# Layer three of a gated feed-forward block in Strassen's form, in passes woven between the steps of layers one and two

## The reference

```
x = x + tanh(g_xattn) * (softmax(Q K^T / sqrt(32)) V Wo + bo)     # Q from layernorm(x), K and V from ctx, 16 heads
h = concat([n, -n]), n = layernorm(x)
h = relu(s0 * h @ sign(k0)) * 2       # layer one:   1024 -> 2048
h = relu(s1 * h @ sign(k1)) * 2       # layer two:   2048 -> 2048
h =      s2 * h @ sign(k2)            # layer three: 2048 -> 512
x = x + tanh(g_ffn) * h
```

## Time and profile before

| | us |
|---|---|
| median of 3 runs | 1567.62 (1564.46 to 1568.11) |
| profiled execution, its own time | 1564.91 |
| its span | 1563.1 |
| PE busy | 1518.9 |
| DVE busy | 940.2 |
| ACT busy | 673.7 |

### The profile page before, as it was taken

How to read it: one execution, slowest core, us unless ns; L and a number is a source line. 1 busy time by engine, 2 the same in 40 slices (tenths; PEclk the granted TensorE clock), 3 DMA queues, 4 the chain that set the end, 5 groups by cost and what they waited for, 6 DMA issues and landing times.

```text
span 1563.1 us, 46137 instructions
## 1 busy us (share of the span) xinstructions
PE 1518.9 (97%) x19872; PEld 1297.3 (83%) x19872; DVE 940.2 (60%) x1938; ACT 673.7 (43%) x1568; POOL 168.7 (11%) x273
## 2 busy tenths in 40 slices
PE   6798999999999999999999999999999999999999
PEld 4586888888888888898988888888898888889887
DVE  5877766756556565655656566465655656565442
ACT  3452452635435253452535445263553525345231
POOL 2202001010100102011020200101010010201000
PEclk9999999999999999999999999999999999999999
DMA  9443232342424333252443524333242443424100
GB/s 256 127 104 58 46 95 62 89 70 62 90 52 101 65 85 78 50 100 55 96 69 71 93 44 103 62 89 69 62 90 52 101 67 83 78 50 100 29 29 15
DMA packets 278227, 120.96 MB, mean 77 GB/s; under 512 B 243464, under 2 KB 259848, under 8 KB 277896
## 3 DMA queue, kind: packets, MB, share of 16 engines
q1 hardware_dynamic: 275960, 117.48, 34.6%
q10 hardware_dynamic: 2064, 0.53, 0.1%
HBM read 37.76 MB, written 16.78 MB: 35 GB/s over the span
## 4 chain that ended last, share of the span: by engine, by line
PE 80%; DVE 8%; ACT 6%; issue 3%; DMA 2%; POOL 0%; SPq 0%; ACTq 0%; DVEq 0%; POOLq 0%
PE bank L1255 19%; PE bank L1256 19%; PE bank L1222 7%; PE bank L1223 7%; PE bank L1272 6%; PE bank L1273 6%; ACT Pf L529 3%; DVE nmax L804 2%; PE bank L1139 2%; PE bank L1141 2%; PE bank L1140 2%; PE bank L1123 2%; PE bank L1124 2%; PE bank L1125 2%; DMA PT<-Phl 1%
## 5 line engine op out<-in xcount | busy, mean ns | idle before, releaser
L1255 PE MATMUL bank<-H,W 128*128 128x128 f16 x6720 | 778.3, 219 | 5.7 <-ACT C L622 4.4
L1256 PE MATMUL bank<-H,W 128*128 128x128 f16 x6720 | 778.0, 219 | 0.0
L1255 PEld LDWEIGHTS bank<-H,W 128*128 128x128 fp8e5 x6720 | 655.3, 98 | 18.1 <-ACT C L622 10.2
L1256 PEld LDWEIGHTS bank<-H,W 128*128 128x128 fp8e5 x6720 | 657.4, 98 | 7.1
L1222 PE MATMUL bank<-hT,W 128*128 128x256 f16 x1024 | 226.8, 273 | 3.5 <-DVE hT L745 1.9
L1223 PE MATMUL bank<-hT,W 128*128 128x256 f16 x1024 | 226.8, 273 | 0.0
L529 ACT ACTIVATE Pf<-bank,nmax 128x128 f32<-128x128 f32 x512 | 146.4, 368 | 137.1 <-DVE nmax L804 135.4
L1273 PE MATMUL bank<-W,h 128*128 128x512 fp8e5 x504 | 191.0, 379 | 0.0
L1272 PE MATMUL bank<-W,h 128*128 128x512 fp8e5 x504 | 191.0, 379 | 0.0
L476 POOL TENSOR_TENSOR attn<-pvs 128x128 f32<-128x128 f32 x120 | 75.0, 625 | 1002.9 <-DVE pvs L817 1002.9
L844 DVE TENSOR_TENSOR C<-bank,C 128x256 f32<-128x256 f32 x180 | 76.3, 424 | 159.4 <-ACT C L622 87.8
(11 more groups left out here) (133 smaller groups left out, 1910.3 us busy)
## 6 DMA issues: line engine op xcount, KB each, us to landing
Qst<-q_bounce SPq DMA_DIRECT2D x120, 128.0 KB, 2.8
Y<-in_x_dram SPq DMA_DIRECT2D x16, 512.0 KB, 3.9
R<-X SPq DMA_DIRECT2D x16, 512.0 KB, 3.5
q_bounce<-Qhl SPq DMA_DIRECT2D x120, 64.0 KB
out_dram<-R SPq DMA_DIRECT2D x15, 512.0 KB, 2.6
W<-in_L_ffn_k_dram SPq DMA_DIRECT2D x8, 512.0 KB, 8.1
W<-in_L_ffn_k_dram SPq DMA_DIRECT2D x2, 1024.0 KB, 19.3
PT<-Phl SPq DMA_TRANSPOSE x120, 3.1
```

What stands on the lines that cost most here:

```text
L1255: mm(o, w, H0[:, 0, i, b_of, :], start=first, stop=False, skip_group_check=True)
L1256: last = mm(o, w, H0[:, 1, i, b_of, :], start=False, stop=i == PAIRS - 1, skip_group_check=True)
```

## The change

Layer three gets Strassen's form too, from chunk 1 on. Two groups make one pass p (groups 0 and 1, or 2 and 3): seven steps of 8 matmuls of 256 columns (`third_step`), in banks 3 and 4 by turns. After a step DVE adds the bank to a quarter of `R` at once (`add_up`, eight reads a pass). Pass 0 lies in slots 31 to 42 of the same chunk, between the steps of L1 of group 2; pass 1 lies in slots 4 to 15 of the next chunk, between the pairs of L0. `SLOTS` grows to 50.

For it the output of layer two must be there in seven rows instead of four quarters: ACT rectifies into `Fp` (`rectify`), DVE makes three sums a group (`group_sums`), ACT converts five and then two rows, 1,280 and 512 elements a partition (`group_hi`), DVE makes the rests of these (`group_lo`); both stand in the slot of P1 of the next group, ACT's before the copy of C11. They replace `h1_rest`.

In L1 the order is now P1, P2, P6, P5, P7, P3, P4, P3 opens bank B anew, which makes a fourth sum a group, and the roles A, B, C move on by one bank from group to group (`ROLES`). PE at the first step of a pass waits for `h2_lo` of the early rows, at the second for the late ones.

The attention items lie in other slots. The sums of signs of `W2` are made in chunk 1 (LATE_WEIGHTS, group 4). In the last chunk groups 2 and 3 are fed to L2 plainly, with a part of `W2` restored. To find the room in SBUF, `Pf` has one buffer instead of two, `attn` shares `xn`, `Qf` shares `pvs`, `ident` and two buffers of the first phase share others, and `Kst` holds one batch of keys (the second is loaded in chunk 7).

The core of the diff, lines left out at "...":

```diff
     A, B, C = range(3)
     STEPS = [(A_L11, B_R11, A, True), (A_L12, B_R21, B, True), (A_S2, B_T2, A, False),
-             (A_S1, B_T1, C, True), (A_S3, B_T3, A, False), (A_L22, B_T4, A, False),
-             (A_S4, B_R22, C, False)]
-    P1, P2, P6, P5, P7, P4, P3 = range(7)
+             (A_S1, B_T1, C, True), (A_S3, B_T3, A, False), (A_S4, B_R22, B, True),
+             (A_L22, B_T4, A, False)]
+    P1, P2, P6, P5, P7, P3, P4 = range(7)
+    ROLES = [[(q + role) % 3 for role in range(3)] for q in range(GROUPS)]
...
+    PASS = [(A_L11, H_R11), (A_L12, H_R21), (A_S2, H_T2), (A_S1, H_T1), (A_S3, H_T3), (A_S4, H_R22), (A_L22, H_T4)]
+    PASS_BANK = [3, 4, 3, 4, 3, 4, 3]
+    READS = [(P1, 0, 1), (P2, 0, 1), (P6, 0, 0), (P5, 1, 0), (P5, 0, 0), (P7, 1, 0), (P3, 0, 0), (P4, 1, 1)]
+    PASS_NEEDS = [0, 0, 1, 2, 3, 5, 6]
+    READ_NEEDS = [0, 1, 0, 0, 3, 4, 5, 0]
...
+    PLAIN_FEED = {0: {0: (0, 0), 1: (0, 1), 3: (1, 0), 4: (1, 1)}, 1: {0: (2, 0), 1: (2, 1), 2: (3, 0), 3: (3, 1)}}
...
-    LAST_FEED = [(1, 0, 1), (1, 1, 2), (0, 1, 0), (0, 0, 3)]
-
-    SLOTS = [("L0", i, 0) for i in range(PAIRS)] + [("L2P", GROUPS - 1, h) for h in range(2)]
-    for q in range(GROUPS):
-        SLOTS += [("L1", q, s) for s in (P1, P2, P6, P5, P7)]
-        SLOTS += [("L2", q - 1, h) for h in range(2)] if q else []
-        SLOTS += [("L1", q, s) for s in (P4, P3)]
+    LAST_FEED = [(0, 1, 0), (1, 0, 1), (0, 0, 2), (1, 1, 3)]
+    SLOTS = [("L0", i, 0) for i in range(4)]
+    for n in range(4):
+        SLOTS += [("L2", 1, n), ("L0", 4 + n, 0)]
+    SLOTS += [("L2", 1, P7), ("L2", 1, P3), ("L1", 0, P1), ("L2", 1, P4)] + [("L1", 0, s) for s in range(P2, 7)]
+    SLOTS += [("L1", 1, s) for s in range(7)] + [("L1", 2, P1), ("L1", 2, P2)]
+    for n, s in enumerate((P6, P5, P7, P3)):
+        SLOTS += [("L2", 0, n), ("L1", 2, s)]
+    SLOTS += [("L2", 0, P7), ("L2", 0, P3), ("L1", 2, P4), ("L2", 0, P4)] + [("L1", 3, s) for s in range(7)]
...
-    for u in range(U):
-        weave(10 + 2 * u, "S", u)
-        weave(11 + 2 * u, "PS", u)
-        weave(15 + 2 * u, "PV", u)
+    for u, (scores, values) in enumerate(((14, 20), (17, 22), (19, 24), (21, 26), (23, 28), (25, 31), (27, 33),
+                                          (29, 36))):
+        weave(scores, "S", u)
+        weave(scores + 1, "PS", u)
+        weave(values, "PV", u)
     for t in range(TT):
-        weave(28 + 2 * t, "CT", t)
-        weave(31 + 2 * t, "WO", t)
-        weave(32 + 2 * t, "N2", t)
-        weave(33 + 2 * t, "T2", t)
-    weave(31, "LOAD", 0)
+        weave(34 + 3 * t, "CT", t)
+        weave(40 + 2 * t, "WO", t)
+        weave(41 + 2 * t, "N2", t)
+        weave(42 + 2 * t, "T2", t)
+    weave(39, "LOAD", 0)
     for t in range(TT):
-        weave(36 + t, "LN", t, 2)
-        weave(38 + t, "N1", t, 2)
-        weave(39 + t, "T1", t, 2)
+        weave(43 + t, "LN", t, 2)
+        weave(45 + t, "N1", t, 2)
+        weave(46 + t, "T1", t, 2)
...
+    LATE_WEIGHTS = ({9: (0, 0), 16: (1, 0), 18: (0, 1), 21: (0, 2), 23: (2, 0), 25: (0, 3), 26: (1, 1), 27: (0, 4),
+                     29: (1, 2), 32: (3, 0), 36: (1, 3), 38: (1, 4), 41: (2, 1), 44: (2, 2), 46: (2, 3), 48: (3, 1)},
+                    {13: (2, 4), 17: (4, 1), 20: (4, 2), 24: (4, 3), 30: (3, 2), 34: (4, 4), 38: (3, 3), 41: (3, 4)})
...
+            def group_hi(q, f):
+                for n, rows in enumerate((EARLY_ROWS, LATE_ROWS)):
+                    act.wait_ge(h2_step, 3 * group(f, q) + 2 + n)
+                    if n == 0:
+                        act.wait_ge(*pass_free(f, q))
+                    nc.scalar.activation(h1[:, q % 2, 0, :, rows, :], Fp[:, 1:3, rows.start + 1:rows.stop + 1, :],
+                                         ACT.Copy).then_inc(h2_hi, 1)
...
                 if kind == "L1":
                     if s == P1:
...
+                        if n > 0 and not late(f, n - 1):
+                            group_hi(n - 1, f)
...
+                        take(n, s, f, C11)
                     if s == P2:
...
+                        act.wait_ge(l1_sum, nth(f - 1, NC, 4 * n))
+                        if n == 0:
+                            act.wait_ge(l0_lo, nth(f, NP, NP - 1))
+                        elif not late(f, n):
+                            act.wait_ge(h2_lo, 2 * group(f, n))
+                        rectify(n, f, 0, H_R11 + 1, C11[:, :, :])
                     if s == P6:
...
+                        if late(f, n - 1):
+                            act.wait_ge(h1_lo, NH + 3)
+                        take(n, s, f, C12)
                     if s == P7:
...
+                        if late(f, n - 1):
+                            act.wait_ge(h1_lo, NH + 2)
+                        take(n, s, f, C22)
+                    if s == P3:
+                        act.wait_ge(l1_sum, nth(f - 1, NC, 4 * n + 2))
+                        rectify(n, f, 1, H_R22 + 1, C22[:, :, :])
                     if s == P4:
+                        act.wait_ge(l1_sum, nth(f - 1, NC, 4 * n + 3))
+                        rectify(n, f, 2, 0, C12[:, :, :])
                         act.wait_ge(l1_done, nth(f, NL1, 7 * n + s))
...
+            def group_sums(q, f):
+                done = 3 * group(f, q)
+                Fg = Fp[:, 1:3]
+                dve.wait_ge(h2_relu, 3 * group(f, q) + 3)
+                V_.tensor_tensor(Fg[:, :, 3:5, :], Fg[:, :, 1:3, :], Fg[:, :, 0:1, :].to_broadcast([P, 2, 2, HALF]),
+                                 ALU.subtract).then_inc(h2_step, 1)
+                dve.wait_ge(h2_step, done + 1)
+                V_.tensor_tensor(Fg[:, :, 5, :], Fg[:, :, 4, :], Fg[:, :, 1, :], ALU.add).then_inc(h2_step, 1)
+                dve.wait_ge(h2_step, done + 2)
+                dve.wait_ge(l1_copy, copied(f, q, 3))
+                V_.tensor_tensor(Fg[:, :, 7, :], Fg[:, :, 6, :], Fg[:, :, 5, :], ALU.subtract).then_inc(h2_step, 1)
+            def group_lo(q, f):
+                for n, rows in enumerate((EARLY_ROWS, LATE_ROWS)):
+                    dve.wait_ge(h2_hi, 2 * group(f, q) + n + 1)
+                    V_.tensor_tensor(h1[:, q % 2, 1, :, rows, :], Fp[:, 1:3, rows.start + 1:rows.stop + 1, :],
+                                     h1[:, q % 2, 0, :, rows, :], ALU.subtract).then_inc(h2_lo, 1)
+            def add_up(f, p, s):
+                base = NR * passes(f, p)
+                for n, (step, half, tile) in enumerate(READS):
+                    if step != s:
+                        continue
+                    if n == 0 and p == 0:
+                        dve.wait_ge(r_copied, nth(f, 16, 15))
+                    if READ_NEEDS[n]:
+                        dve.wait_ge(l2_sum, base + READ_NEEDS[n])
+                    dve.wait_ge(l2_step, 7 * passes(f, p) + s + 1)
+                    rest = R[:, tile, half * CHUNK:(half + 1) * CHUNK]
+                    V_.scalar_tensor_tensor(out=rest, in0=banks[PASS_BANK[s]][:, 0:CHUNK], scalar=fin, in1=rest,
+                                            op0=ALU.mult, op1=ALU.add).then_inc(l2_sum, 1)
...
+                if kind == "L2" and f - n >= 1:
+                    add_up(f - n, n, s)
...
+                    banks_of = ROLES[n]
+                    if s == P1 and n > 0 and not late(f, n - 1):
+                        group_lo(n - 1, f)
                     if s == P2:
...
+                        dve.wait_ge(l1_copy, copied(f, n, 0))
+                        add(n, s, f, C11, banks_of[B])
+                    if s == P6 and late(f, n):
+                        last_rest(n, 0, C11[:, :, :])
+                    if s == P5:
+                        dve.wait_ge(l1_copy, copied(f, n, 1))
+                        add(n, s, f, C12, banks_of[C])
                     if s == P7:
...
+                        dve.wait_ge(l1_copy, copied(f, n, 2))
+                        add(n, s, f, C22, banks_of[C])
                     if s == P3:
...
+                        dve.wait_ge(l1_sum, nth(f - 1, NC, 4 * n + 1))
+                        add(n, s, f, C12, banks_of[B])
+                        if late(f, n):
+                            last_rest(n, 1, C22[:, :, :])
+                    if s == P4 and late(f, n):
+                        last_rest(n, 2, C12[:, :, :])
+                        last_rest(n, 3, banks[banks_of[A]][:, 0:CHUNK].rearrange("p (j n) -> p j n", j=2))
+                    if s == P4 and not late(f, n):
+                        group_sums(n, f)
...
                     if s == P1 and n > 0:
-                        pe.wait_ge(h1_lo, nth(f, NH, 4 * (n - 1) + 2))
-                    if s == P2 and n > 0:
-                        pe.wait_ge(l1_sum, nth(f - 1, NC, 3 * (n - 1)))
+                        pe.wait_ge(l1_sum, nth(f - 1, NC, 4 * (n - 1) + 3))
                     if s == P6:
-                        pe.wait_ge(l1_copy, nth(f - 1, NC, 3 * n))
-                    if s == P5 and n > 0:
-                        pe.wait_ge(l1_sum, nth(f - 1, NC, 3 * (n - 1) + 2))
```

(35 more changed lines are left out.)

320 lines of the change are left out of this document (181 added, 139 removed).

## The result

The changed kernel takes 1642.54 us (median of 4 runs, 1640.23 to 1643.11) against 1567.31 us for the kernel before (4 runs). The ratio is 1.0481, interval 1.0462 to 1.0499: slower by 75 us. The forecast was slower by 43 us, 1611 us with a range to 1628. So the sign is right and the size is not. The profiled execution took 1643.0 us.

What follows compares the result with a forecast made beforehand. PE's matmul order was taken as the bound, with ACT and DVE's 0.4 us slack a round deciding. 1564.9 - 23.1 - 9.1 + 57.4 + 14.3 + 6 - 0.4 = 1610.0, plus 1: 1611 us, forecast range 1592 to 1628, wider range 1562 to 1628.

Steps and rivals of the forecast that it cites:

- The undisturbed period: Regular chunk at full clock, first pair to next chunk's first pair: forecast 95.7 us, 92.66 us in the kernel before.
- What bounds the kernel: Steady state: PE, busy 97%, sets the time by its matmul order; a change is worth its columns and waits.
- the slack of 0.4 us a round: Attention exchange in L1 of groups 0 and 1: ACT and DVE need 3.63 us a round, PE 4.04 us.
- Columns, -0.80 us a pass: Layer three: 56 matmuls of 256 columns replace 32 of 512, 6.11 for 6.91 us; 29 passes give -23.1 us.
- Old waits, -0.65 us a chunk: Short waits before P4 and P6 vanish with rotating banks and P4 after P3: -9.1 us over 14 chunks.
- The walk through groups 0 and 1, +4.1 us: PE waits at P6 (1.37) and P7 (0.8) of group 1 and slot 31 (1.93 us): +57.4 us in 14 chunks.
- The chunk's end, 1.1 us: P4 of group 3 waits 0.4 us, the first L0 step 0.7, behind N1 and T1: +14.3 us over 13 chunks.
- The clock: Rival "more waiting": a 2 us PE wait in every chunk could lower the clock; above 1628 us, chance 0.05.
- Chunk 0 costs nothing: Chunk 0, among other parts of the change, costs nothing that PE waits for: 0 us.
- Chunk 1, +6 (2 to 9) for the `W2` sums: Chunk 1 also makes W2's four sums; about 9.5 us before slot 31 meet some 4 us of slack.
- the 4 us of slack: Chunk 1 before slot 31: slack set against about 9.5 us of sums of signs, leaving +6 us.
- First phase, nothing: Aliases in the first phase cost nothing that PE waits for; PE there waits for attention, which they don't lengthen.

Runs made afterwards that it cites:

- the narrow groups: Changed kernel with group sums, conversions and rests on 16 of 128 columns, output left incomplete: 1547.96 us, ratio 0.9874.
- the banks alone: Kernel before, layer three not in Strassen's form, with only P3 before P4, a fourth C sum a group and rotating banks: 1561.76 us, ratio 0.9966.
- the part on GpSimd: Changed kernel with the third group sum and the rest of the late rows moved from DVE to GpSimd: 1630.88 us, ratio 1.04.
- the pass later: Changed kernel with pass 0 starting one L1 step later, behind P6 of group 2: 1624.14 us, ratio 1.0361.
- all four edits: Changed kernel with pass 0 one step later, chunk 0's sums of signs earlier, third sum and late rests on GpSimd, score items moved: 1601.08 us, ratio 1.021.
- the copy first: Changed kernel with ACT's C11 copy of the next group ahead of the two group conversions: 1662.87 us, ratio 1.0605.
- the chunk's end earlier: Changed kernel with the layernorm items LN, N1 and T1 one slot earlier: 1642.29 us, ratio 1.0481.
- the sums in chunk 0: Changed kernel with W1 sums earlier, plus three W2 sums of signs moved from chunk 1 to chunk 0: 1639.23 us, ratio 1.0451.
- the one with a gap of 1.76 us: Changed kernel with group operations on 16 of 128 columns, plus a PE gap before slot 31 from six GpSimd additions: 1579.59 us, ratio 1.0076.

## Why the prediction was right in sign and wrong in size

The waits and their places were right; the size failed in four terms. A lower clock behind slot 31 and any loss in chunk 0 were put at nothing and cost 9.6 and 3.9 us. The sums of signs in chunk 1 were put at 6 us and cost 12. The undisturbed period was put at +2.95 us a chunk and came out at +3.75. Another 3.25 us go with the execution. By its own steps:

- **What bounds the kernel: right.** PE's order sets the time, and the slack of 0.4 us a round on ACT and DVE decides.
- **Columns, -0.80 us a pass: right** (-1.55 us for two passes, from the narrow groups against the banks alone). The weights stay hidden: a step of a pass still takes 0.87 us.
- **Old waits, -0.65 us a chunk: right** (92.00 for 92.66).
- **The walk through groups 0 and 1, +4.1 us: nearly right.** P6 1.36 for 1.37, P7 0.81 for 0.8, slot 31 2.30 for 1.93. The prices of the unseen operations were 1.27 (1.270 measured) and 1.48 us (1.545). The third stop came out 0.37 too small.
- **The chunk's end, 1.1 us: 1.39** (0.46 and 0.93). With slot 31 and the columns (0.05 less than forecast) that is 0.7 of the 0.8 us by which an undisturbed chunk is longer than the terms say (+3.75 for +2.95); 0.1 has no place found. Over 13 chunks it is about 10 us. (The prediction's period of 95.7 us is 95.6 by its own terms.)
- **The clock: the step that failed in kind.** The fall behind the slot-31 wait was named as a rival and set aside, since the first 20 us of the kernel before, with PE busy for 8.84, show 1.00. That row stands for the launch and not for a gap inside a stream. Six chunks at 1.6 us make 9.6 us; the part on GpSimd, which has no such fall, is shorter by just that in chunks 2 to 14. The Trainium skill (TensorE: Matmul & The Clock Gate, HAM oscillation — how this bites in real kernels) tells of a kernel whose waits for data send the clock to its lower level time and again. The runs here show the same behind gaps of PE of 1.95 us and more, and behind none of 42 gaps of 1.91 us or less.
- **"Chunk 0 costs nothing": wrong by 3.9 us.** It had 3.45 us less for PE to do, and ran no shorter. The `W1` sums at slots 44 to 48 stand before the rest that PE's first L0 step needs, and that wait is 5.9 us for the 1.6 of the kernel before. Moved forward they gave back 2.2 us of the 3.9 in chunk 0 (3.0 with chunk 1); after that PE waits for `xT`.
- **Chunk 1, +6 (2 to 9) for the `W2` sums: 12 measured.** Chunk 1 makes eight sums of signs; the five in slots 13 to 30 are three of `W2` and two of `W1`. P6 of group 1 waits 3.97 us in it, with the lower clock behind. The step that failed is the 4 us of slack set against these sums. The narrow groups keep the sums of signs and have next to no work for the rows, and their chunk 1 still takes 101.07 us, where their undisturbed chunk, with one pass in Strassen's form in place of two, would take 90.45 + 0.80. So the signs cost 9.8 us there, with waits of 1.0, 1.5 and 1.9 us and one fall of the clock, and 109.89 - 96.41 - 0.80 = 12.7 us with the rows at full width. The likely reason, which no run tests by itself, is that a sum of 2.3 us comes in one piece and is longer than the slack between two hand-offs. With three of them taken out, chunk 1 was 3.2 us shorter.
- **First phase, nothing:** +3.25 us, in this execution. It shows a clock of 0.96 there for the 1.00 of the kernel before, and the kernel with the banks alone has 0.95 and +2.0, while the runs with the pass later and with all four edits have no such delay (73.8 us at clock 1.00). It goes with the execution and not with the change.

In chunks 2 to 14 the clock (9.6) and the longer period (10.4) make 20 us, of which about 1 comes back in chunk 14 and in shorter waits for DMAs. 3.25 + 3.9 + 6.1 + 19.0 + 0.95 = 33 us, the distance from 1610.0 to 1643.0. The structure of the waits was read rightly from the trace before. The forecast's range was too narrow at the top because each term was summed at its middle, while what a full chain adds (the clock behind a long wait, an operation longer than the slack it falls into) only ever added here.

## What to carry to other kernels

Saving columns on a TensorE that is 97% busy pays only if the operations that feed the new form fit between the others' hand-offs: walk one period of the serving engines in order, at the place where they are fullest, and don't go by their mean share. When the walk finds a wait of TensorE of about 2 us or more, add the clock behind it (here 1.6 us in half of the cases at 2.1 us), and first move the step until the wait is split or gone: with the pass one slot later chunks 2 to 14 took 19.8 us less, 11 by the waits and most of the rest by the clock. Compare a long operation with the one gap that it falls into, not with the sum of the slack around it. Moving a delay within a chain that is full (the copy first, the chunk's end earlier, the sums in chunk 0) gave it back elsewhere in all three runs. Work handed to GpSimd is priced with what it takes from VectorE while both run.

## What the runs showed of the hardware

- Idle times of TensorE of 1.10 to 1.91 us, once a period of 90 to 99 us, left the granted clock at 1.00 in 42 of 42 chunks. Of 2.08 to 2.15 us, 23 of 45 were followed by a lower clock, of 2.52 us 9 of 11, of 2.92 to 3.08 us 12 of 13. In the rows shown 4.6 us from the pass's first step on are at 0.63, a mean of a part at full and a part at half speed (the two levels are 2.4 and 1.2 GHz). A fall cost 1.6 us.
- On GpSimd the rest of 512 elements took 1.80 us in the mean, where its addition of 512 from `Y` and `bo_b` takes 1.27 us and DVE needs 0.68. The 14 that overlap DVE's N1 took 1.16 us (and N1 1.37), the 44 beside DVE's rest of the early rows or a sum in `Fp` took 1.94 us or more.
- The other way round, a DVE sum of 256 elements from SBUF took 0.42 us, and 1.38 us where it overlapped GpSimd's rest (14 of 14).
- A layernorm step of one element a partition on GpSimd (`var_eps`) took 0.26 us in the mean in the kernel before, 0.86 us in the changed one and 0.20 in the one with a gap of 1.76 us. The traces show what it overlaps. It takes 0.19 us alone or beside a DVE sum that reads a PSUM bank (L844, 14 of 14), 0.54 us beside DVE's group sum (L957) and 1.34 us beside its rest of 1,280 elements (L968), 14 times each. So DVE's new operations hold it up, and a mean over all its cases hides that. In the kernel with a gap these DVE operations are narrow, and it takes 0.19 us beside them.
